# A three-layer interaction network on one core: layer 0's pair sums as three fp32r products, with the halves made by ScalarE and GpSimd

## What is computed

```python
e = stack([tbl_f[ids[:, f]] for f in range(39)], axis=1)     # (1024, 39, 16)
xk = e
for W in (f0, f1, f2):                                        # (39*39,128), (128*39,128), (128*39,128)
    z = einsum('bfd,bgd->bfgd', e, xk).reshape(b, f * g, d)
    xk = einsum('bpd,pm->bmd', z, W)
    outs.append(xk)
h = concatenate([sum(concatenate(outs, 1), -1), dense_ctx], axis=1)
h = relu(h @ W_top1 + b_top1); h = relu(h @ W_top2 + b_top2); y = h @ W_top3
```

## Time and profile before

| | us |
|---|---|
| median of 3 runs | 1411.15 (1411.0 to 1412.47) |
| profiled execution | 1398.14 |
| its span, first to last instruction | 1396.1 |
| busy PE | 1320.1 (95%) |
| busy VectorE | 1125.4 (81%) |
| busy ScalarE | 908.1 (65%) |
| busy GpSimd | 703.1 (50%) |

### The profile page before, as it was taken

The page is one execution under the profiler, slowest core; times in us unless marked ns, Lnnn a source line. Parts: engine busy times, 40 slices in busy tenths (PEclk is TensorE's granted clock), DMA queues, the critical chain, the costliest instruction groups (busy, mean ns, idle before and its releaser), DMA issues.

```text
span 1396.1 us, 20072 instructions
## 1 busy us (share of the span) xinstructions
PE 1320.1 (95%) x5856; PEld 992.7 (71%) x5856; DVE 1125.4 (81%) x2792; ACT 908.1 (65%) x3233; POOL 703.1 (50%) x697
## 2 busy tenths in 40 slices
PE   1199999999999999999999999999999999999998
PEld 0166766777777777777777777777777777777777
DVE  0279988888878888788878888788887888788874
ACT  1157777677666766667666776667666677667663
POOL 6786556654645466554556546454664532233200
PEclk8599999999999999999999999999999999999998
DMA  5271021100311021110211003110221102110000
GB/s 108 48 212 38 13 76 43 50 27 8 98 37 36 20 69 51 35 41 2 84 35 49 27 3 102 31 41 21 60 59 35 42 1 74 40 47 26 1 1 1
DMA packets 51355, 62.47 MB, mean 45 GB/s; under 512 B 12707, under 2 KB 24725, under 8 KB 51245
## 3 DMA queue, kind: packets, MB, share of 16 engines
q1 hardware_dynamic: 33644, 54.64, 12.7%
q0 software_dynamic: 10128, 2.98, 2.0%
q10 hardware_dynamic: 7473, 3.56, 1.0%
HBM read 10.02 MB, written 0.00 MB: 7 GB/s over the span
## 4 chain that ended last, share of the span: by engine, by line
PE 88%; DVE 4%; POOL 3%; ACT 2%; issue 2%; DMA 1%; SPq 0%; DVEq 0%
PE Y L740 20%; PE Y L742 19%; PE Y L741 19%; PE C L688 14%; PE C L702 5%; PE S L696 5%; POOL rows L331 3%; ACT Y L467 2%; PE C L720 1%; PE C L710 1%; PE C L711 1%; PE S L662 1%; DVE sum_b L607 1%; ACT h L474 1%; DVE sum_a L612 1%
## 5 line engine op out<-in xcount | busy, mean ns | idle before, releaser
L467 ACT ACTIVATE Y<-Y,x_col 128x128 f32<-128x128 f32 x2944 | 800.9, 356 | 402.8 <-PE Y L742 388.3
L740 PE MATMUL Y<-f_high,cur_high 128*128 128x512 f32 (+1 forms) x1280 | 627.7, 490 | 9.3 <-DVE part L620 4.6
L742 PE MATMUL Y<-f_high,cur_low 128*128 128x512 f32 (+1 forms) x1280 | 498.3, 389 | 0.0
L741 PE MATMUL Y<-f_low,cur_high 128*128 128x512 f32 (+1 forms) x1280 | 497.6, 389 | 0.0
L369 POOL TENSOR_TENSOR pairs<-shifted,base 117x512 f32<-117x512 f32 x186 | 240.3, 1294 | 471.5 <-PE C L688 469.6
L331 POOL DMA_INDIRECT rows<-in_tbl_dram,ids_sb x312 | 304.6, 976 | 77.0 <-issue 65.2
L740 PEld LDWEIGHTS Y<-f_high,cur_high 128*128 128x128 f32 x1280 | 241.0, 188 | 122.9 <-issue 46.3
L741 PEld LDWEIGHTS Y<-f_low,cur_high 128*128 128x128 f32 x1280 | 242.1, 189 | 92.3 <-issue 52.2
L742 PEld LDWEIGHTS Y<-f_high,cur_low 128*128 128x128 f32 x1280 | 240.3, 188 | 51.1
L607 DVE SCALAR_TENSOR_TENSOR sum_b<-Y,x_col,sum_b 128x128 f32<-128x128 f32 x768 | 262.6, 342 | 0.0
L688 PE MATMUL C<-pairs,f_sum 117*128 117x512 f32 (+1 forms) x448 | 230.0, 596 | 6.1 <-DVE pairs L570 6.1
(11 more groups left out here) (78 smaller groups left out, 649.2 us busy)
## 6 DMA issues: line engine op xcount, KB each, us to landing
shifted<-x_seq SPq DMA_DIRECT2D x157, 234.0 KB
base<-x_seq SPq DMA_DIRECT2D x95, 78.0 KB
rows<-in_tbl_dram,ids_sb POOLq DMA_INDIRECT x312
shifted<-x_seq SPq DMA_DIRECT2D x31, 156.0 KB
...
```

What stands on the lines that cost most here:

```text
L467: ins = act.activation(where[:, i * M:(i + 1) * M], where[:, i * M:(i + 1) * M], ACT.Copy, scale=x_col[:, t // JT % QG, t % JT, f:f + 1])
L740: pe.matmul(where, ch, wh, start=True, stop=False)
L741: pe.matmul(where, ch, wl, start=False, stop=False)
L742: pe.matmul(where, cl, wh, start=False, stop=True).then_inc(y_filled, 1)
```

## The change

Layer 0's seven sums are each three fp32r products of halves, as layer 1's are: `f0_sum` and `f0_low` are the filter's halves (made once at the start by ScalarE and VectorE), `pairs_high` and `pairs_low` the pair's. For each pair GpSimd multiplies into `pairs` (a ring of two now), ScalarE rounds to `pairs_high` (`round_pair`), GpSimd subtracts to `pairs_low` (`pair_low`), and TensorE does three products. The waits follow: a pair waits for the low two before, a low for its rounding, a rounding for its pair and for the sum three before, a sum for its low.

The tables that set the places change too: sums stand in slots 9, 12, 16, 20, 24, 27 and 31 (12, 15, 18, 22, 25, 28 and 31 in groups with the tower); roundings stand on ScalarE behind slots 1, 5, 9, 11, 15, 19 and 21 (1, 5, 9, 14, 15, 19 and 25). The split moves on ScalarE from chunk 31 to 35, on VectorE behind the first four fused steps after the second reduce. Gathers are dealt 2, 3, 2, 4 to the tiles of a group. Besides, the accumulators lose their second buffer, the tower's `h1`, `h2` and `y` lie in `rows_seq`, and ScalarE sends each batch step's output itself.

```diff
-AT_SUM = [12 + 3 * k for k in range(K0)]
+AT_SUM = [9, 12, 16, 20, 24, 27, 31]
+AT_SUM_MLP = [12, 15, 18, 22, 25, 28, 31]
+AT_ROUND = [1, 5, 9, 11, 15, 19, 21]
+AT_ROUND_MLP = [1, 5, 9, 14, 15, 19, 25]
+GATHER_SHARE = (2, 3, 2, 4)
...
-    u, tiles = u - 2, TPB - 2
-    if step + 1 >= BT or u < 0:
+    if step + 1 >= BT or u < 2:
         return None
-    return step + 1, range(NF * u // tiles, NF * (u + 1) // tiles)
+    share = [GATHER_SHARE[(v - AHEAD) % JT] for v in range(2, TPB)]
+    done, all_ = sum(share[:u - 2]), sum(share)
+    return step + 1, range(NF * done // all_, NF * (done + share[u - 2]) // all_)
...
             def pair(g, k):
-                pool.wait_ge(cur0_summed, z - RING + 1)
...
+                if g == 1 and k < PAIR_RING:
+                    pool.wait_ge(first_low, K0)
+                else:
+                    pool.wait_ge(low_ready, z - K0 - PAIR_RING + 1)
...
+            def pair_low(g, k):
+                z = K0 * g + k
+                r = K0_ROWS[k]
+                pool.wait_ge(pairs_rounded, z + 1)
+                pool.tensor_tensor(pairs_low[0:r, z % RING, :], pairs[0:r, z % PAIR_RING, :],
+                                   pairs_high[0:r, z % RING, :].bitcast(F32), ALU.subtract).then_inc(low_ready, 1)
+
+            LOW_STEPS = ((("pair", 0), ("pair", 1), ("low", 0), ("pair", 2), ("low", 1)),
+                         (("low", 2), ("pair", 3), ("low", 3), ("pair", 4)),
+                         (("low", 4), ("pair", 5), ("low", 5), ("pair", 6), ("low", 6)),
+                         ())
...
-                    ks = ((0, 1, 2), (3, 4), (5, 6), ())[j] if g + 1 < NG else ()
...
+                    steps = LOW_STEPS[j] if g + 1 < NG else ()
...
+            def round_pair(g, k):
+                z = K0 * g + k
+                r = K0_ROWS[k]
+                if g:
+                    act.wait_ge(pairs_ready, z - K0 + 1)
...
+                if z >= RING:
+                    act.wait_ge(cur0_summed, z - RING + 1)
+                act.activation(pairs_high[0:r, z % RING, :], pairs[0:r, z % PAIR_RING, :], ACT.Copy)\
+                   .then_inc(pairs_rounded, 1)
...
                         if c == 1:
...
-                            if j == JT - 1 and g + 1 < NG:
-                                split_cur0(g + 1)
...
                         if c == AT_G:
+                            if j == JT - 1 and g + 1 < NG:
+                                split_cur0(g + 1)
...
+                        if CH * j + c in rounds_in_group(g) and g + 1 < NG:
+                            round_pair(g + 1, rounds_in_group(g).index(CH * j + c))
...
-                if j == JT - 1 and g + 1 < NG:
-                    split_cur0(g + 1)
                 dve.wait_ge(scaled, NSC * t + 4)
-                dve.tensor_reduce(part[:, t % 2, :], unit(t, 2), AX.X, ALU.add).then_inc(acc_steps, 1)
-                fuse(t, 6, FUSE6, 1)
+                dve.tensor_reduce(part[:], unit(t, 2), AX.X, ALU.add).then_inc(acc_steps, 1)
+                fuse(t, 6, FUSE6, 1)
+                if j == JT - 1 and g + 1 < NG:
+                    split_cur0(g + 1)
                 fuse(t, 7, FUSE7, 1)
...
-                    pe.wait_ge(pairs_ready, z - K0 + 1)
+                    pe.wait_ge(low_ready, z - K0 + 1)
...
-                pe.matmul(C[:], f0_sum[0:r, k, :], pairs[0:r, z % RING, :],
-                          start=k == 0, stop=k == K0 - 1).then_inc(cur0_summed, 1)
+                high, low = pairs_high[0:r, z % RING, :], pairs_low[0:r, z % RING, :]
+                pe.matmul(C[:], f0_sum[0:r, k, :], high, start=k == 0, stop=False)
+                pe.matmul(C[:], f0_low[0:r, k, :], high, start=False, stop=False)
+                pe.matmul(C[:], f0_sum[0:r, k, :], low, start=False, stop=k == K0 - 1).then_inc(cur0_summed, 1)
```

More of the change, by code:

```diff
@@ L107, in mlp_in_group, with sums_in_group, rounds_in_group @@
     return BT - 2 if g == NG - 1 else None
+def sums_in_group(g):
+    return AT_SUM_MLP if mlp_in_group(g) is not None else AT_SUM
+def rounds_in_group(g):
+    return AT_ROUND_MLP if mlp_in_group(g) is not None else AT_ROUND
 def mlp_tile(g):
@@ L165, in build @@
         shifted = sb("shifted", [SEL, K0 - 1, GN])
-        pairs = sb("pairs", [SEL, RING, GN])
+        pairs = sb("pairs", [SEL, PAIR_RING, GN])
+        pairs_high = sb("pairs_high", [SEL, RING, GN], F32R)
+        pairs_low = sb("pairs_low", [SEL, RING, GN], F32R)
         cur0_high = sb("cur0_high", [P, 2, GN], F32R)
@@ L170, in build @@
         x_col = sb("x_col", [P, QG, JT, FC])
-        sum_a = sb("sum_a", [P, 2, M])
-        sum_b = sb("sum_b", [P, 2, M])
-        part = sb("part", [P, 2, M])
+        sum_a = sb("sum_a", [P, M])
+        sum_b = sb("sum_b", [P, M])
+        part = sb("part", [P, M])
         cur1 = sb("cur1", [P, 2, M])
@@ L395, in _ @@
                             take_rows(bt + 1, part)
-                    ks = ((0, 1, 2), (3, 4), (5, 6), ())[j] if g + 1 < NG else ()
-                    for i in range(max(len(ks), len(fs))):
-                        if i < len(ks):
-                            pair(g + 1, ks[i])
+                    steps = LOW_STEPS[j] if g + 1 < NG else ()
+                    for i in range(max(len(steps), len(fs))):
+                        if i < len(steps):
+                            kind, k = steps[i]
+                            (pair if kind == "pair" else pair_low)(g + 1, k)
                         if i < len(fs):
@@ L484, in read_y @@
                 act.wait_ge(m3_filled, n)
-                act.activation(y[:, bt * P:(bt + 1) * P], C[0:1, 0:P], ACT.Copy).then_inc(c_read, 1)
-            read_scalars(0)
+                if bt:
+                    act.wait_ge(y_out, 16 * bt)
+                act.activation(y, C[0:1, 0:P], ACT.Copy).then_inc(c_read, 1)
+                act.wait_ge(c_read, C_USE["mlp", bt, 2] + 1)
+                act.dma_start(out[bt * P:(bt + 1) * P, :].rearrange("b o -> o b"), y).then_inc(y_out, 16)
+            read_scalars(0)
+            act.wait_ge(f0_ready, 2)
+            act.activation(f0_sum[:, 0:K0 - 1, :], f0_direct[:, 0:K0 - 1, :], ACT.Copy).then_inc(f0_high_ready, 1)
+            r = K0_ROWS[K0 - 1]
+            act.activation(f0_sum[0:r, K0 - 1, :], f0_direct[0:r, K0 - 1, :], ACT.Copy).then_inc(f0_high_ready, 1)
+            for k in range(K0):
+                round_pair(0, k)
             read_scalars(1)
@@ L569, in _ @@
                     shift = shifted[0:r, k - 1, :]
-                dve.tensor_tensor(pairs[0:r, k % RING, :], shift, base[0:r, 0, :], ALU.mult).then_inc(first_pairs, 1)
+                if k >= PAIR_RING:
+                    dve.wait_ge(first_low, k - PAIR_RING + 1)
+                dve.tensor_tensor(pairs[0:r, k % PAIR_RING, :], shift, base[0:r, 0, :], ALU.mult).then_inc(first_pairs, 1)
+                if k:
+                    first_pair_low(k - 1)
+            first_pair_low(K0 - 1)
             def split_cur0(g):
@@ L593, in fuse @@
                 for i, f in enumerate(CH_F[c]):
-                    acc = (sum_a if c < 4 else part, sum_b)[(i + starts) % 2][:, t % 2, :]
+                    acc = (sum_a[:] if c < 4 else part[:], sum_b[:])[(i + starts) % 2]
                     src = bank(t, c)[:, i * M:(i + 1) * M]
@@ L611, in tile @@
                 dve.wait_ge(scaled, NSC * t + 2)
-                dve.tensor_reduce(sum_a[:, t % 2, :], unit(t, 0), AX.X, ALU.add).then_inc(acc_steps, 1)
+                dve.tensor_reduce(sum_a[:], unit(t, 0), AX.X, ALU.add).then_inc(acc_steps, 1)
                 fuse(t, 2, FUSE2, 0)
@@ L625, in tile @@
                 dve.wait_ge(acc_steps, n0 + FUSE7 + 2)
-                dve.tensor_tensor(b_and_a, b_and_a, sum_a[:, t % 2, :], ALU.add).then_inc(acc_steps, 1)
+                dve.tensor_tensor(b_and_a, b_and_a, sum_a[:], ALU.add).then_inc(acc_steps, 1)
                 dve.wait_ge(scaled, NSC * t + 6)
                 dve.wait_ge(acc_steps, n0 + JOIN)
-                dve.tensor_tensor(bank(t, 9)[:, SUM_SLOT * M:], b_and_a, part[:, t % 2, :], ALU.add)\
+                dve.tensor_tensor(bank(t, 9)[:, SUM_SLOT * M:], b_and_a, part[:], ALU.add)\
                    .then_inc(acc_steps, 1)
@@ L788, in _ @@
                         g_product(t - 1)
[L789 to L790 removed]
+                    if s in sums_in_group(g) and g + 1 < NG:
+                        cur0_sum(g + 1, sums_in_group(g).index(s))
                     if s == AT_SCALARS and g + 2 < NG:
```

66 lines of the change are left out of this document (42 added, 24 removed).

## The result

The changed kernel takes 1599.8 us (median of 4 runs, 1595.6 to 1615.7) against 1411.1 for the kernel before: a ratio of 1.136, 95% interval 1.128 to 1.144. That is 189 us slower. I had said 122 slower, 1533, within 1490 to 1575, and 1600 as the upper end if the clock fell.

A forecast was written before the change was run, and what follows sets the result against it. TensorE was taken to set the pace, 38.3 of a group's 39.5 us. Added losses 95 + 7 + 15 + 1 + 4 = 122 us on 1398.14 gave 1520; the median, 13 higher, gave 1533, range 1490 to 1575.

The forecast's parts named there:

- 118: Predicted loss in the 31 groups: 95 for groups 5 to 24, 7 group 25, 15 groups 0 to 4, 1 the last.
- The gain: TensorE's seven sums per group go from 0.86 to 0.70 us each: 1.1 us a group, 35 us in all.
- The turns: Tiles 1 and 2: GpSimd and ScalarE alternate, gathers between, from rounding 2 on; 4.1 us lost before chunk 26.
- the walk: One q=3 group followed from its first layer 2 product at 0 to VectorE reaching tile 3 at 37.25 us.
- The split moved back: Group's end: VectorE splits 6.25 us after tile 3's first reduce instead of 3.40, so the next group starts at 43.7.
- The other groups: Added us: q=1 +6.8, q=2 and q=0 +4.0 each, groups 0 to 4 15, groups 26 to 30 +1 together.
- Rival 4: TensorE's clock falls to half for one 6.5 us stretch, costing some 3 us, 26 times: 1610; chance 12%.
- Rival 2: Gathers cost the turns nothing, falling into the roundings; all groups like the last five: 1424; chance 6%.
- rival 1: Faster as meant: turns hidden, split in time, TensorE stays the bound: 1380; chance 7%.
- Start and end: Before group 0, +4 us from VectorE's subtractions and f0's low half; output DMAs on ScalarE below 1 us each.
- The rule on two-input work: Two-input elementwise work belongs on VectorE, GpSimd being about half as fast (0.69 against 1.29 us); sum left unchanged.

The follow-up runs named there:

- e12: The kernel before, unchanged, profiled a second time beside the other runs: 1407.25 us.
- e11: Changed kernel with split at its old places, GpSimd's pairs ahead of unneeded low halves, two pairs made a tile ahead, row copies all in last tile: 1401.5 us.
- e9: Changed kernel with only GpSimd's order in tiles 1 and 2 altered, pairs 3 to 6 each ahead of low 2 to 5: 1524.2 us.
- e3: Changed kernel with layer 2's slices and the tower's first products one slot later, so chunk 0 comes first in a group: 1551.3 us.
- e1: Changed kernel without the row gathers of batch tiles 2 to 7: 1479.2 us.
- e4: Changed kernel with 14 extra TensorE products at two waits per group, ahead of the first chunk and of chunk 26: 1590.4 us.

## Why the prediction was right, and where it was not

Against e12 the changed kernel's profile is 194.4 us longer in its span: 3.4 at the start, 189.5 in the 31 groups (1444.4 for 1254.9), 1.5 behind them. I had 4 and 118.

**The gain.** Right in size: three products 0.23 us apart stand in the trace (670.28, 670.51, 670.74), and e11 shows 1.4 us per group where I took 1.1.

**The turns.** Right, by mechanism and by clock time. From 982.94 rounding 2 ends at 12.6 (worked out: 12.6), pair 3 at 16.4 (16.4), pair 4 at 21.3 (21.2), rounding 5 at 26.5 (26.25); `sum_a` is done at 29.75 and chunk 26 starts at 29.8 (29.8). Behind it this group runs 3.4 us at half clock, and tile 3's first reduce comes at 38.5 instead of the 37.25 worked out. In group 23, of the same kind but without a spell, it comes at 37.25:

```profile
1176.46 1.13 PE L786 MATMUL C<-G,f_sb 128*128 128x128 f32 x8 [1.68 <-DVE z L658]
...
1213.71 1.22 DVE L694 TENSOR_REDUCE sum_a<-Y 128x128 f32<-128x1024 f32 x1
```

So the walk holds to its end at full clock. e9 shows the cause: only the order changes, and ScalarE's waits for pairs fall from 192.6 to 72.4 us. What I did not see in it is that the order was needless, since pair 3 does not depend on low 2; I took it as the cost of the work.

**The split moved back.** Here lies the failed step: "the next group starts at 37.25 + 6.25 + 0.2 = 43.7". The 6.25 is right (6.24 in the group shown), but two terms that belong beside it stand at nothing. The first is `z`. The step ends TensorE's wait with `cur_low`; the products that stand first in 27 groups, layer 2's and the tower's, write the bank that `z` is still being read from, so they wait for `z` as well, 0.7 us more, 18 us in all (shown by the groups at full clock in e3 and the changed kernel). The second and larger is the clock. The step takes TensorE at full clock, at the group's start and in the turns, and I had left the fall to a rival. By the prices of a spell read within one execution, 0.33 to 0.46 of its length, the 143.4 us cost 47 to 66; that is an estimate. With the 18 of `z` it makes 65 to 84 for the 71.5 us by which the 31 groups exceed my 118. e3 takes `z` and the spells at the groups' starts away together and comes to 1551 us; its q0 and q3 are then 48.0 and 43.7, the forecast's. For q3 that was worked out; q0's 4.0 was only taken over from q3, so its agreement is in part luck.

**The other groups.** Even e3 is 23 us above the 118 (its 31 groups take 1396.1): 8 in groups 0 to 4, where I had 15 and it is 23.6, 7 in q1 (47.5 for 46.3) and 7 in q2 (45.8 for 44.5). Much of this is the clock in the turns. The one q2 group of e3 without a spell takes 44.35, three with a spell of 3.4 us take 45.9 and one with 6.8 takes 47.2. In q1 every group has a spell, so there the price of the row copies, 2.6 in my sum, can't be told from the clock's. Groups 2 and 4, which have none, take 41.7 and 41.6 where I had 40.8.

**Rivals.** Rival 4, the falling clock, is in the main what came: its 1610 is the forecast and 78 us more, and I had given it 12%. My reason for the low chance was a wait of 1.2 us that left the clock at 1.00; behind the waits of 1.7 to 2.0 us for `z` it fell in 13 of 27 places. I had counted one stretch a group; the spells stand in two places, at the start and in the turns. The Trainium skill's "TensorE: Matmul & The Clock Gate", in "HAM oscillation — how this bites in real kernels", prices a spell at half of its length. The tower groups come near it: a spell of 10.2 us costs 4.2 within e1, 4.3 by e4 and 4.6 by e3 (5.3 less 0.7 of `z`). Rival 2 (gathers free) is out by e1, and rival 1 (1380) needed all four edits of e11 to come as far as 1401.

**Start and end.** Right: 3.4 and 1.5 us against 4 in all. The rule on two-input work that the prediction cites from the Trainium skill's "GPSIMD Engine Reference", section 4.1, did not decide: GpSimd's subtraction takes 1.29 us and VectorE's, in the first group, 0.69, a ratio that agrees with the rule, and yet e11 leaves the halves on GpSimd and is faster than before. No run moved them to VectorE.
